# Attention scores of two heads side by side on TensorE's row groups, with a longer lead of the query scores

## The chip, the cores and the metric

The kernel runs on one core of one Trainium2 chip. The metric is the device time of one execution in microseconds (us); three runs of a kernel are given with their median.

## The reference

A macaron layer on x of shape 8 x 256 x 128 (2048 tokens of 128 features, fp32): half a mixture-of-experts stage, an attention, and half a second expert stage with the same weights.

```
ffn(x):  p = softmax(x @ w_gate + b_gate);  e = argmax(p)          # 8 experts, one per token
         y = relu(x @ W1[e] + b1[e]) @ W2[e] + b2[e];  return y * max(p)      # 128 -> 512 -> 128
attn(x): xn = x * rsqrt(mean(x*x) + 1e-6) * norm_w
         q, k, v = xn @ Wq.T + bq, xn @ Wk.T + bk, xn @ Wv.T + bv   # 16 heads of 8 features
         s = q @ k.T / sqrt(8), -inf above the diagonal             # 256 x 256 for each head
         return xn + softmax(s) @ v @ Wo.T + bo
x = x + 0.5 * ffn(ln(x));  x = x + attn(ln(x));  x = x + 0.5 * ffn(ln(x))    # ln: layer norm
```

## The kernel before

**Stages.** A first expert stage, the projections to queries, keys and values, the attention, the routing of the second expert stage (which begins beside the end of the attention), and the second expert stage with POOL's indirect DMAs (dispatch, L479). Each engine has its own instruction list in an order written out by hand; semaphores join them.

**Split numbers.** Queries and keys are split into three bf16 parts each, so that a bf16 product over 6 x 8 = 48 rows (BLK x HD = JROWS) gives a head's score to nearly fp32 precision. Two heads lie above each other in the 96 rows (SROWS) of the stack buffers qz and ks, which SP loads from DRAM (stack_load, L395) with four DMAs for each half of a sequence. In qz the rows of the other head hold zeros, so that a product over 96 rows gives one head. There are two pairs of stack buffers, one for each of two sequences.

**Steps and units.** The attention goes through 16 steps: 8 sequences, each in two halves of 8 heads. This document numbers them 0 to 15; step n is half n % 2 of sequence n // 2. A step has six units u = 0 to 5. A unit fills one PSUM bank of 128 x 512 twice over: with key-major scores (scores_k, L1410) of this step, and with query-major scores (scores_q, L1383) of the step two later, which serve to find each query's row maximum. Units 0, 1, 3 and 4 hold the first 128 keys of a pair of heads against all 256 queries (and the last 128 queries against all keys); units 2 and 5 hold the remaining 128 x 128 blocks of four heads.

**The way of a maximum.** In the query scores TensorE first writes the causal mask into the bank as a product of the identity with a mask table (L1393, L1401), then adds the scores (L1396, L1405). VectorE takes the maximum along the keys (max_unit, L1049, one tensor_reduce of 128 x 512 for a unit). After six units POOL splits the 16 maxima of a query into three bf16 parts (max_split, L544, five small operations), TensorE transposes them into bank 6 (turn_max, L1453, after unit 2), ScalarE copies them to mT (L753), and SP writes them by DMA as three more rows of qz (max_rows, L408). Key scores are a product over these 99 rows, so the maximum is already subtracted in the bank.

**The way of the scores.** ScalarE takes the exponential of a key-score bank to the SBUF tile pT (exp_unit, L740); the two key-score banks alternate. POOL zeroes the entries above the diagonal with affine_select (mask, L562): four masks of 128 x 512 in a step, each after the units that it covers (units 0 and 1; 2; 3 and 4; 5). TensorE multiplies with the values (pv, L1431): part 0 (units 0 to 2) stands after unit 4, part 1 (units 3 to 5) after unit 1 of the next step. An exponential waits until the P·V that read its pT slot before is done. POOL also carries three residual operations (residual, L512, 128 x 256) for each sequence: after masks 1 and 3 of an even step and mask 1 of an odd step (RES_AT, L62).

**The output of a sequence**, one sequence later: ScalarE's out_copy (L755); TensorE's turn_out (L1461) after units 4 and 5 of the even step, into banks 7 and 6; VectorE's normalise (L1094) after unit 5 of the even and unit 0 of the odd step; turn_norm (L1469) after unit 2 and project (L1475) after unit 4 of the odd step; VectorE's add_out (L1104) after its unit 5. VectorE also spreads the values of the next sequence (v_spread, L1088) in the even step. add_out of sequences 0 to 7 is what the second routing (layer norm, gate products, route pick, slots) starts from; late_routing (L1524) puts TensorE's part of it into steps 14 and 15. POOL's first dispatch stands behind its masks of step 15.

**Banks.** 0 and 1 query scores, 2 and 3 key scores, 4 and 5 P·V, 6 and 7 the transposes and projections.

**Loops.** Steps 2 to 9 run in a hardware loop of two turns on every engine; POOL has a small operation in front of each mask there ("turn", L569).

The core of TensorE's step:

```
for u in range(6):
    scores_k(b, k, half, u)
    if more: scores_q(b + 1, bh, 1 - k, half, u)
    if u == 1 and half: pv(b, k, 0, 1)
    elif u == 1 and not first: pv(b - 1, 1 - k, 1, 1)
    if u == 2: ...turn_max...
    if u == 4: pv(b, k, half, 0)
```

Of the kernel before, what the change touches and what calls it, by code (L numbers as in the profile page):

```python
# [67 lines left out]
SROWS = 2 * JROWS  # L68
MROW = SROWS
KROWS = MROW + 3  # L70
NEG1_PAIR = -1082081408
LN_EPS, RMS_EPS = 1e-5, 1e-6
NEG = -1e30
SCALE = 1.0 / float(np.sqrt(np.float32(HD)))
# [28 lines left out]
def build(nc, x_in, wqkvo, cols_in, rows_in, w_gate, experts_in, const_in, out):  # L103
    ctx = ExitStack()
    with ctx:
# [40 lines left out]
        gT = sb("gT", [P, 2, 512])  # L146
# [33 lines left out]
        low = sb("low", [P, P])  # L180
        xs_sb = sb("xs_sb", [P, RING, RW])
# [9 lines left out]
        xnT = sb("xnT", [P, 2, 4 * P])  # L191
        qkr = sb("qkr", [P, 2, 2, 4 * P])
# [8 lines left out]
        mb = sb("mb", [P, 2, 2, 3, 8], BF16)  # L201
        turn = sb("turn", [P, 4])
# [67 lines left out]
        x_ld = sems("x_reloaded", NQ)  # L270
# [13 lines left out]
        low_s = sem("keep_table_set")  # L284
        q_std = sems("sequence_splits_stored", B)
        a_va = sem("attn_v_spread")
        a_stk = [sems(f"stack_loaded{i}_", 2) for i in range(2)]
# [20 lines left out]
        def need(eng, s, n):  # L308

            if not isinstance(n, int) or n > 0:  # L310
                eng.wait_ge(s, n)
# [8 lines left out]
        def scattered(f, k, n):  # L320

            return 16 * (f * len(range(k, NS, OUT)) + n)

# [17 lines left out]
        def _(sp):  # L341
# [53 lines left out]
            def stack_load(b, k, half):  # L395

                r0 = b * (2 * t_rows)
                if half == 0:
                    sp.wait_ge(q_std[b], 64)
                need(sp, a_st, 12 * (b - 2) + 6 * half + 6)  # L400
                for j in range(2):
                    rows_j = slice(JROWS * j, JROWS * (j + 1))
                    for t, buf in ((0, qz[k][rows_j, half, j, :, :]),
# [4 lines left out]
            def max_rows(b, k, half):  # L408

                sp.wait_ge(a_mtc, 2 * b + half + 1)  # L410
                sp.dma_start(qz[k][MROW:MROW + 3, half, :, :, :].rearrange("s j i n -> s (j i n)"), mT[:, half, :]
                             ).then_inc(a_m[half], 16)
# [3 lines left out]
            for q in range(NQ):  # L416
                sp.dma_start(x[:, 4 * q:4 * q + 4, :], tok_view(x_d, q)).then_inc(x_ld[q], 16)
            sp.wait_ge(static_s, 6)
            split_stores(0, 1)
            stack_load(0, 0, 0)  # L420
            stack_load(0, 0, 1)
            stack_load(1, 1, 0)
            max_rows(0, 0, 0)
# [18 lines left out]
        def _(pool):  # L442
# [134 lines left out]
            def step(b, half, more=True):  # L577
                if half == 0:
                    max_split(b, 1)
                elif more:  # L580
                    max_split(b + 1, 0)
# [1044 lines left out]
```

## Time and profile before

| | before |
|---|---|
| median of 3 runs | 317.94 us (317.46 to 318.11) |
| profiled execution | 317.4 us, span 315.3 us |
| TensorE busy | 271.4 us (86%) |
| VectorE busy | 212.2 us (67%) |
| POOL busy | 185.7 us (59%) |
| ScalarE busy | 149.2 us (47%) |

The span runs from the first to the last instruction of the profiled execution; its own time is what that execution took as a run. "Busy" is the time in which an engine computes; waiting and issuing are not in it. PE is TensorE, DVE VectorE, ACT ScalarE, POOL GpSimd, SP the queue that issues most DMAs. PEclk is the granted clock of TensorE as a share of full speed. In a row in order of time the first two numbers are the start and the length of an instruction in us; matmuls are pipelined, so their lengths overlap and the distance from start to start is what one costs its engine. "xN" joins N instructions to one row. Step 0 starts at 123.58 us, step 2 at 137.05, step 13 at 212.28, step 14 at 219.33.

### The profile page before, as it was taken

The page shows a single profiled execution, that of the slowest core. Times are in us where ns is not written, and L with a number is a line of the kernel's source. Part 1 is how long each engine was busy: PE and PEld are TensorE (multiplying, and loading weights), DVE is VectorE, ACT ScalarE, POOL GpSimd, SP SyncE. Part 2 cuts the span into 40 slices and gives each one's busy share as a digit, 9 for nine tenths or more (in the row PEclk, how much of TensorE's full clock was granted, in tenths as well). Part 3 has the DMA queues.
Part 4 walks back from the last instruction along what each step waited for, and adds up shares of the span by engine and source line. Part 5 has one row for each costly group of instructions (what it writes and reads, how often), then busy time and mean ns, then how long its engine had stood idle before and what let it go on. Part 6 is the DMA issues. An engine that isn't in the chain of part 4 may idle for free.

```text
span 315.3 us, 7921 instructions
## 1 busy us (share of the span) xinstructions
PE 271.4 (86%) x2368; PEld 219.5 (70%) x2368; DVE 212.2 (67%) x685; ACT 149.2 (47%) x362; POOL 185.7 (59%) x332
## 2 busy tenths in 40 slices
PE   7724999999997778999989999998977759999980
PEld 6724999999994544656656565665646658999970
DVE  4956058888539568986657777776587744888860
ACT  2300076666206613676656667666541007666620
POOL 7587815445726313786767787888647740555561
PEclk9999999999999996999999999999976799999997
DMA  6974232221041733552433522110001143122100
GB/s 184 397 313 122 60 80 55 68 67 32 17 133 41 202 109 112 165 166 87 135 95 115 157 74 70 58 55 2 5 10 45 56 113 91 49 68 67 30 21 0
DMA packets 34388, 29.37 MB, mean 93 GB/s; under 512 B 4109, under 2 KB 28818, under 8 KB 34353
## 3 DMA queue, kind: packets, MB, share of 16 engines
q1 hardware_dynamic: 29696, 23.52, 25.1%
q0 software_dynamic: 2496, 4.27, 4.3%
q10 hardware_dynamic: 2160, 1.14, 1.4%
q8 instruction: 18, 0.29, 0.4%
q14 instruction: 18, 0.14, 0.1%
HBM read 17.08 MB, written 12.55 MB: 94 GB/s over the span
## 4 chain that ended last, share of the span: by engine, by line
PE 48%; POOL 16%; issue 9%; DMA 9%; DVE 9%; SPq 4%; ACT 2%; POOLq 1%; ACTq 0%; DVEq 0%
PE bank L1291 12%; PE bank L1302 11%; POOL disp_d L479 7%; PE bank L1448 4%; PE bank L1420 3%; PE bank L1396 3%; POOL pT L574 2%; PE bank L1426 2%; DMA row<-in_x 2%; PE bank L1393 2%; SPq L406 2%; POOL row L470 2%; PE bank L1283 2%; PE bank L1401 2%; DMA disp_d<-row,slot 2%
## 5 line engine op out<-in xcount | busy, mean ns | idle before, releaser
L746 ACT ACTIVATE pT<-bank 128x512 f32<-128x512 f32 x96 | 56.5, 600 | 43.0 <-PE bank L1426 29.2
L1056 DVE TENSOR_REDUCE mh<-bank 128x2 f32<-128x512 f32 x64 | 42.1, 683 | 10.1 <-PE bank L1396 9.9
L1302 PE MATMUL bank<-experts,hT 128*128 x368 | 48.9, 276 | 0.0
L1291 PE MATMUL bank<-xsT,ew 128*128 128x128 f32 x368 | 48.8, 276 | 0.1
L1222 PE MATMUL bank<-zero 128*128 128x128 f32 x268 | 37.3, 305 | 10.5 <-DVE rowi L934 4.7
L574 POOL TENSOR_SCALAR_AFFINE_SELECT pT<-pT 128x512 f32<-128x512 f32 x62 | 40.2, 651 | 9.4 <-ACT pT L746 9.3
L1302 PEld LDWEIGHTS bank<-experts,hT 128*128 128x128 f32 x368 | 44.8, 192 | 0.5 <-issue 0.3
L1291 PEld LDWEIGHTS bank<-xsT,ew 128*128 128x128 f32 x368 | 44.7, 192 | 0.5 <-issue 0.2
L1222 PEld LDWEIGHTS bank<-zero 128*128 128x128 f32 x268 | 35.8, 219 | 11.0 <-DVE rowi L934 4.7
L664 ACT ACTIVATE hT<-bank,ew 128x128 f32<-128x128 f32 x92 | 28.9, 365 | 28.7 <-PE bank L1291 28.7
L941 DVE TENSOR_SCALAR hT<-bank,ew 128x128 f32<-128x128 f32 x92 | 28.0, 346 | 21.3 <-PE bank L1291 19.9
L479 POOL DMA_INDIRECT disp_d<-row,slot x32 | 32.3, 1009 | 13.3 <-issue 13.3
L487 POOL DMA_INDIRECT out<-ys_sb,xs_sb x23 | 22.6, 983 | 29.2 <-DVE ys_sb L965 27.7
L487 POOL DMA_INDIRECT x_d<-ys_sb,xs_sb x23 | 22.8, 991 | 24.1 <-DVE ys_sb L965 22.8
L652 ACT ACTIVATE xq<-xs_sb 128x128 f32<-128x128 f32 x46 | 22.5, 492 | 28.8 <-DMA xs_sb<-disp_d 28.8
L1060 DVE TENSOR_REDUCE mh<-bank 128x4 f32<-128x512 f32 x32 | 22.1, 690 | 19.3 <-PE bank L1405 19.3
L1420 PE MATMUL bank<-qz,ks 99*128 99x512 bf16 x64 | 24.8, 390 | 1.9 <-DMA qz<-mT 1.7
L1396 PE MATMUL bank<-ks,qz 96*128 96x256 bf16 x128 | 25.4, 281 | 0.0
L949 DVE TENSOR_SCALAR ew<-experts 128x644 f32 x46 | 22.4, 494 | 2.4 <-issue 1.8
L1448 PE MATMUL bank<-pT,va 128*32 128x256 f32 x256 | 20.9, 398 | 1.8 <-DVE pT L1182 1.5
L957 DVE TENSOR_TENSOR yb<-bank,ew 128x128 f32<-128x128 f32 x46 | 13.4, 292 | 12.8 <-PE bank L1302 10.0
L1393 PE MATMUL bank<-cb 128*128 128x256 bf16 x64 | 18.1, 283 | 1.6 <-DMA ks<-sp_d 1.3
(140 smaller groups left out, 465.9 us busy)
## 6 DMA issues: line engine op xcount, KB each, us to landing
sp_d<-spl SPq DMA_DIRECT2D x32, 192.0 KB, 2.5
experts<-in_experts SPq DMA_DIRECT2D x8, 578.0 KB, 9.5
qz<-sp_d SPq DMA_DIRECT2D x32, 96.0 KB
ks<-sp_d SPq DMA_DIRECT2D x32, 96.0 KB
xs_sb<-disp_d SPq DMA_DIRECT2D x46, 66.0 KB, 1.9
row<-in_x SPq DMA_DIRECT2D x4, 256.0 KB, 5.2
row<-x_d SPq DMA_DIRECT2D x4, 256.0 KB, 3.6
disp_d<-pad ACTq DMA_DIRECT2D x12, 66.0 KB
```

The lines of the kernel that those rows point to most:

```text
L479: pool.indirect_dma_start(disp_d[f][:, :], bass.IndirectOffsetOnAxis(ap=slot[:, t:t + 1], axis=0), row[:, t, :], None).then_inc(d_tok[f], 16)
L487: pool.indirect_dma_start(target[:, :], bass.IndirectOffsetOnAxis(ap=xs_sb[:, t % RING, ID:ID + 1].bitcast(U32), axis=0), ys_sb[:, t % OUT ...
L574: pool.affine_select(out=p_, in_=p_, pattern=[[0, 4], [1, P]], compare_op=ALU.is_ge, fill=0.0, base=0, channel_multiplier=-1).then_inc(a_p ...
L664: mm = act.activation(hT[:, par, c, :], bank[2 + 2 * par][:, c * P:(c + 1) * P], ACT.Relu, bias=ew[:, k, HID + c:HID + c + 1])
L746: act.activation(pT[:, u, :], bank[2 + u % 2][:, :], ACT.Exp, scale=SCALE).then_inc(a_e, 1)
L1056: dve.tensor_reduce(mh[:, half, 1, :, 2 * pp + w], bank[u % 2][:, :].rearrange("p (h n) -> p h n", h=2), AX.X, ALU.max).then_inc(a_mx, 1)
L1222: pe.matmul(bank[b][:, 0:P], zero[:, :], zero[:, :], start=True, stop=True)
L1291: mm = pe.matmul(bank[2 + 2 * (k % 2) + c // 2][:, (c % 2) * P:(c % 2 + 1) * P], ew[:, k % WRING, c * P:(c + 1) * P], xsT[:, k % 2, :], st ...
L1302: mm = pe.matmul(bank[6 + k % 2][:, 0:D], hT[:, k % 2, c, :], w2.rearrange("p a c -> p (a c)"), start=(c == 0), stop=(c == HC - 1))
L1396: mm = pe.matmul(ov[:, j, :], qz[k][0:SROWS, half, j, pair - 4 * half, P:T], ks[k][0:SROWS, pair, :], start=False, stop=True, **MM_BANK)
L1420: mm = pe.matmul(ov, ks[k][0:KROWS, pair, 0:P], qz[k][0:KROWS, half, :, pair - 4 * half, :], start=True, stop=True, **MM_BANK)
L1448: mm = pe.matmul(o[32 * h:32 * h + 32, pp * T:(pp + 1) * T], va[:, k, 0, 8 * j + pair, :], pT[:, 3 * pp + h // 2, j * T:(j + 1) * T], star ...
```

## The change

**Row groups.** The two heads of a pair no longer share rows: head 0 lies at partitions 0 to 47, head 1 at 64 to 111, each followed by its own three rows of maxima (48 to 50, 112 to 114; max_rows becomes two DMAs). A product is over 48 or 51 rows, and a unit now interleaves a key-score product of one row group with a query-score product of the other (scores). The zeros in qz are dropped. Units 2 and 3 are now the ones with 128 x 128 blocks of four heads, units 0, 1, 4 and 5 the wide ones with two products each.

**Lead.** Three pairs of stack buffers, three query banks (0, 1, 6). From step 2 on a step computes the query scores of step n + 3 (QUERY_OF); between steps 1 and 2 the query half 4 is computed alone (scores_alone); steps 13 to 15 have none. The row maxima are turned two steps ahead (MAX_OF), after unit 3.

**Mask.** In the wide units, from sequence 1 on, the mask product is dropped; VectorE adds the mask from a table msk and takes the maximum in one operation (tensor_tensor_reduce, 128 x 256, two for a unit). Units 2 and 3, and all units of sequence 0, keep the mask product and tensor_reduce.

**Moves.** P·V part 0 stands after unit 5 and waits for three masks, part 1 for all five; POOL has five masks (three of 512 columns, two of 256) and a max_split of four operations; its residual stays behind masks 1, 3 and 1. Bank 6 being a query bank, turn_out uses bank 7 twice: first query block after unit 5 of the even step, second after unit 1 of the odd step, where it waits for normalise of the first. turn_norm, project and add_out follow at units 0, 1 and 2 of the next even step. The maxima's transposes use bank 7. One value-bias addition (quad_vbias(3)) and the mask table go to VectorE's prologue. All loops are unrolled and the turn operations dropped.

```diff
@@ constants
-KROWS = MROW + 3
+KROWS = JROWS + 3
+JBASE = P // 2
+QB = (0, 1, 6)
+QUERY_OF = [n + 2 if n < 2 else n + 3 for n in range(HALVES - 3)] + [None] * 3
+MAX_OF = [n + 1 if n < 2 else n + 2 for n in range(HALVES - 2)] + [None] * 2
...
-        qz = [sb(f"qz{i}", [P, 2, 2, 4, T], BF16) for i in range(2)]
-        ks = [sb(f"ks{i}", [P, NPAIR, T], BF16) for i in range(2)]
+        qz = [sb(f"qz{i}", [P, 2, 4, T], BF16) for i in range(3)]
+        ks = [sb(f"ks{i}", [P, NPAIR, T], BF16) for i in range(3)]
...
@@ POOL
+            def mask(n, i):
+                pool.wait_ge(a_e, 6 * n + (2, 3, 4, 5, 6)[i])
...
+                pool.affine_select(out=p_, in_=p_, pattern=[[0, 2 if i > 2 else 4], [1, P]], compare_op=ALU.is_ge,
+                                   fill=0.0, base=0, channel_multiplier=-1).then_inc(a_pm, 1)
+            def step(n):
...
+                for i in range(5 if n < HALVES - 1 else 2):
+                    mask(n, i)
...
+                    elif (half, i) in RES_AT:
+                        residual(b, RES_AT.index((half, i)))
@@ ScalarE, exp_unit
-                need(act, a_pv, 2 * (2 * b + half - 1) + 1 + u // 3
+                need(act, a_pv, 2 * (2 * b + half - 1) + (1 if u < 2 else 2)
@@ VectorE, max_unit
+                if b == 0 or late:
+                    i1 = dve.tensor_reduce(top, bank[QB[u % 3]][:, :].rearrange("p (h n) -> p h n", h=heads),
+                                           AX.X, ALU.max)
...
+                    for m in range(heads):
+                        sc = bank[QB[u % 3]][:, m * n:(m + 1) * n]
+                        i1 = dve.tensor_tensor_reduce(sc, sc, msk[:, T - n:T], 1.0, LOWEST, ALU.add, ALU.max,
+                                                      top[:, m:m + 1])
@@ VectorE, step
+                    if (half, u) == (0, 2):
+                        if b >= 2:
+                            add_out(b - 2)
+                        v_spread(b + 1, (b + 1) % 2)
...
+                        if (half, u) == (1, 0):
                             normalise(b - 1, 0)
-                        if half == 1 and u == 0:
+                        if (half, u) == (1, 2):
                             normalise(b - 1, 1)
@@ TensorE
+            def scores(n, mq, u):
+                if u == 0:
+                    pe.wait_ge(a_m[n % 2], 32 * (n // 2 + 1))
+                need(pe, a_e, 6 * n + u - 1)
+                if mq is not None:
+                    scores_q_waits(mq, u)
+                    masked = mq < 2 or unit(u)[0]
+                    if masked:
+                        scores_q_mask(u)
+                for m in range(unit(u)[2]):
+                    mm = scores_k_part(n, u, m)
+                    if mq is not None:
+                        mm_q = scores_q_part(mq, u, m, masked)
...
             def pv(b, k, half, pp):
-                pe.wait_ge(a_pm, 8 * b + 4 * half + 2 * pp + 2)
+                pe.wait_ge(a_pm, 5 * (2 * b + half) + 3 + 2 * pp)
...
             def step(n):
                 for u in range(6):
+                    scores(n, QUERY_OF[n], u)
+                    if (half, u) == (0, 0) and b >= 2:
+                        turn_norm(b - 2)
+                    if u == 1 and n > 0:
+                        pv(b if half else b - 1, b % 2 if half else 1 - b % 2, 1 - half, 1)
+                    if (half, u) == (0, 1) and b >= 2:
+                        project(b - 2)
+                    if u == 3 and MAX_OF[n] is not None:
...
+                        turn_max(MAX_OF[n])
+                    if u == 5:
+                        pv(b, b % 2, half, 0)
...
+                    if (half, u) == (0, 5) and 1 <= b and not last:
+                        pe.wait_ge(a_mtc, MAX_OF[n] + 1)
+                        turn_out(b - 1, 0)
+                    if (half, u) == (1, 1) and 1 <= b and not last:
+                        pe.wait_ge(a_an, 2 * b - 1)
+                        turn_out(b - 1, 1)
+                    if last:
+                        if (half, u) == (0, 4):
+                            pe.wait_ge(a_x, b - 1)
+                            turn_out(b - 1, 0)
+                        if (half, u) == (1, 0):
+                            pe.wait_ge(a_an, 2 * b - 1)
+                            turn_out(b - 1, 1)
...
+            for u in range(6):
+                scores_alone(4, u)
```

## Rows read from the trace of the kernel before

**Rows 1.** Busy time of each engine in four stretches; columns in its first line.

```profile
...
core 0: us, PE busy (x) PEld busy (x) DVE busy (x) ACT busy (x) POOL busy (x), PEclk, DMA share, GB/s
123.58:137.05 13.47, 13.08 (x122) 8.01 (x121) 11.93 (x19) 8.95 (x16) 9.58 (x21) 0.88 0.61 176
137.05:212.28 75.23, 73.23 (x783) 46.24 (x784) 53.88 (x116) 47.96 (x94) 57.60 (x153) 1.00 0.34 100
212.28:219.33 7.05, 6.51 (x72) 4.17 (x70) 4.78 (x11) 4.20 (x9) 5.64 (x13) 1.00 0.01 2
219.33:233.44 14.11, 12.09 (x123) 8.07 (x124) 9.87 (x40) 8.53 (x18) 7.80 (x17) 0.97 0.01 3
```

**Rows 2.** Waits, 137.05 to 212.28 us: waiter, releaser, us, times, longest.

```profile
...
ACT pT L746 <- PE bank L1426: 18.9, 23, 1.0
...
PE bank L1420 <- DMA qz<-mT: 1.7, 1, 1.7
```

**Rows 3.** TensorE in order of time, steps 2 and 3: start, us, line, operation.

```profile
...
138.09 0.38 PE L1396 MATMUL bank<-ks,qz 96*128 96x256 bf16 x2
138.41 0.64 PE L1448 MATMUL bank<-pT,va 128*32 128x256 f32 x8
138.86 0.40 PE L1444 MATMUL bank<-pT,va 128*32 128x128 f32 x8
139.20 0.39 PE L1426 MATMUL bank<-qz,ks 99*128 99x256 bf16 x2
139.43 0.38 PE L1401 MATMUL bank<-cb 128*128 128x512 bf16 x1
...
142.19 0.66 PE L1465 MATMUL bank<-ident_t,oT 128*128 128x128 f32 x4
142.68 0.38 PE L1426 MATMUL bank<-qz,ks 99*128 99x256 bf16 x2
...
149.25 0.71 PE L1478 MATMUL bank<-wt,anT 128*128 128x128 f32 x4
149.79 0.39 PE L1426 MATMUL bank<-qz,ks 99*128 99x256 bf16 x2
```

**Rows 4.** VectorE in order of time, from 143 to 153 us.

```profile
...
143.55 0.69 DVE L1060 TENSOR_REDUCE mh<-bank 128x4 f32<-128x512 f32 x1 [1.04 <-PE bank L1405]
144.16 0.25 DVE L1098 RECIPROCAL rl<-bank 128x16 f32<-128x16 f32 x1
144.44 0.29 DVE L1100 TENSOR_TENSOR an<-bank,rl 128x128 f32<-128x128 f32 x1
...
151.27 0.41 DVE L1107 TENSOR_TENSOR row<-bank,row 128x256 f32 x1
151.60 1.28 DVE L1056 TENSOR_REDUCE mh<-bank 128x2 f32<-128x512 f32 x2
```

**Rows 5.** ScalarE and POOL in order of time, step 3.

```profile
...
143.10 0.60 ACT L746 ACTIVATE pT<-bank 128x512 f32<-128x512 f32 x1 [0.84 <-PE bank L1426]
...
143.78 0.20 POOL L569 TENSOR_TENSOR turn<-zero 128x1 f32<-128x1 f32 x1 [0.58 <-ACT pT L746]
143.93 0.64 POOL L574 TENSOR_SCALAR_AFFINE_SELECT pT<-pT 128x512 f32<-128x512 f32 x1
...
144.53 0.72 POOL L521 TENSOR_TENSOR res<-res,rows 128x256 f32<-128x256 f32 x1
...
145.21 0.22 POOL L552 TENSOR_TENSOR mb<-mh,zero 128x16 bf16<-128x16 f32 x1
```

**Rows 6.** VectorE and POOL in order of time, steps 14 and 15 and after.

```profile
...
220.14 0.41 DVE L1107 TENSOR_TENSOR row<-bank,row 128x256 f32<-128x256 f32 x1
...
227.11 0.22 DVE L861 TENSOR_TENSOR lg<-bank,row 128x64 f32<-128x64 f32 x1 [1.20 <-PE bank L1252]
...
229.84 0.25 DVE L1098 RECIPROCAL rl<-bank 128x16 f32<-128x16 f32 x1
...
233.44 1.09 POOL L479 DMA_INDIRECT disp_d<-row,slot  x1 [1.78 <-issue]
```

More of the change, by code:

```diff
@@ L577, in step @@
[L577 to L581, printed above, removed]
-                for n in range(4 if more or half == 0 else 2):
-                    mask(b, half, n // 2, n % 2)
-                    if isinstance(b, int) and b >= 6:
-                        if b == 6 and n > 0:
-                            residual(6 + half, n - 1)
-                    elif (half, n) in RES_AT:
-                        residual(b, RES_AT.index((half, n)))
-                    if isinstance(b, int) and b >= 5 and (half, n) == (0, 1):
+                z_ = zero[:, 0:16].rearrange("p (q j h) -> p q j h", q=2, j=2)
@@ L594, in _ @@
             quad_repeat(4, 1)
-            for half in range(2):
-                if half == 1:
-                    quad_repeat(4, 0)
-                step(0, half)
-            with pool.Fori(0, 2) as i:
-                for k in range(2):
-                    for half in range(2):
-                        step(2 * i + 1 + k, half)
-            for b in (5, 6, 7):
-                for half in range(2):
-                    step(b, half, more=b < 7)
+            step(0)
+            quad_repeat(4, 0)
+            step(1)
+            max_split(3)
+            for n in range(2, HALVES):
+                step(n)
             dispatch(1, 0, range(0, 3))
@@ L785, in _ @@
             quad_split2(4)
-            step(0, 1, True, first=True)
-            with act.Fori(0, 2) as i:
-                for k in range(2):
-                    for half in range(2):
-                        step(2 * i + 1 + k, half, True)
-            for b in (5, 6, 7):
-                for half in range(2):
-                    step(b, half, b < 7)
+            step(1)
+            max_copy(3)
+            for n in range(2, HALVES):
+                step(n)
             out_copy(7, 1)
@@ L1148, in _ @@
             for u in range(6):
-                max_unit(0, 1, u)
+                max_unit(1, u)
             v_spread(0, 0)
-            for half in range(2):
-                step(0, 0, half, True, first=True)
-            with dve.Fori(0, 2) as i:
-                for k in range(2):
-                    for half in range(2):
-                        step(2 * i + 1 + k, 1 - k, half, True)
-            for b in (5, 6):
-                for half in range(2):
-                    step(b, b % 2, half, True)
+            step(0)
+            step(1)
+            for u in range(6):
+                max_unit(4, u)
+            for n in range(2, HALVES - 2):
+                step(n)
+            add_out(5)
             def late_stats(q):
@@ new lines, in scores_q_waits, with scores_q_part @@
+                    pe.wait_ge(a_stk[mq // 2 % 3][mq % 2], 64 * (mq // 6 + 1))
+                need(pe, a_mx, 6 * mq + u - 2)
+            def scores_q_part(mq, u, m, masked=False):
+                late, p0, heads = unit(u)
+                n = 512 // heads
+                q_, k_ = head(mq // 2 % 3, mq % 2, p0 + m, 1 - u % 2, JROWS)
+                return pe.matmul(bank[QB[u % 3]][:, m * n:(m + 1) * n], q_[:, 0:P] if late else q_[:, P:T], k_[:, 0:n],
+                                 start=not masked, stop=True, **(MM_BANK if masked else {}))
@@ L1518, in step @@
                             turn_norm(b - 1)
[L1519 removed]
+                        if (half, u) == (1, 4):
                             project(b - 1)
[L1521 removed]
                         late_routing(half, u)
```

411 lines of the change are left out of this document (191 added, 220 removed).

## The prediction

> **What bounds the kernel now.** I read the busy shares first, then busy time by stretch, then the waits, then TensorE, VectorE and POOL in order of time. TensorE is busy 86% of the span, but the stretch decides, not the share. Steps 2 to 12 of the attention (a step is one half of the heads of one sequence) take 75.23 us, TensorE is busy in 73.23 of them, and VectorE, ScalarE and POOL in 46 to 58 [rows 1]. The 2.0 us without TensorE are nearly all one wait of 1.7 for the row-maximum transfer; ScalarE's exponentials wait 18.9 us for TensorE's scores [rows 2]. So 75.23 − 1.7 = 73.5 us over 11 steps is 6.68 a step, set by TensorE's stream. The changed kernel takes work out of that stream; the question is what is late next. Behind the attention POOL's dispatches and the second expert stage run in series, so what comes late at the first dispatch (233.44 [rows 6]) comes late at the end.
>
> **TensorE's stream.** Two products of 256 columns take .23 (139.20 to 139.43 [rows 3]), so one takes .11. A unit (key scores, mask, query scores) costs .34 to .45 of it now. Side by side on two row groups it costs .22, and .44 where the mask stays (units 2 and 3). That is 4 × .22 + 2 × .44 = 1.76 a step in place of about 2 × (.22 + .34 + .22 + .34 + .22 + .45) = 3.6, or 1.8 less. The trace has no pair on two row groups. Its nearest case is eight products of 256 columns on four column groups that take .45 (138.41 to 138.86 [rows 3]) where eight in turn would take .9; so tiles do run beside each other, and I take the full overlap. The other bound is none.
>
> **What a step waits for then.** I cost the 1.8 at nothing gained by itself and follow the chain, since P·V of units 0 and 1 now stands after unit 5 and needs three POOL masks, and the exponentials of the next step's units 0 and 1 need that P·V. Prices: P·V .79 (138.41 to 139.20), turn_out .49 (142.19 to 142.68), turn_norm half of that, .25, project .54 (149.25 to 149.79), score start to exponential .42 and so .20 after a .22 unit, all [rows 3] with the exponential at 143.10 [rows 5]; exponential .60 long, .08 to POOL's next start (143.70 to 143.78), mask .60 start to start and .64 long, residual .68 (144.53 to 145.21) [rows 5]; normalise .28 + .29 [rows 4]. A switch between the tile shapes: P·V starts at 138.41, the two products before it end at 138.09 + .22 = 138.31, so .10 [rows 3].
>
> *Odd step, from its first score:* two units .44, P·V .79: 1.23. turn_out of the second query block now shares bank 7 with the first and waits for VectorE's normalise, which stands behind unit 0's maximum: .42 + two reduces of .42 (below) + .57 + .05 = 1.88. Queued behind that wait on TensorE is unit 2, and behind it exponential 2. turn_out to 2.37; unit 2 with mask and switch .54, 2.91; exponential 3.11 to 3.71; second mask 3.79; residual 4.39, third mask 5.07 to 5.71; P·V 5.76 to 6.55.
>
> *Even step:* .22 + .25 + .22 + .79 + .54 = 2.02; unit 2 to 2.56; exponential 2.76 to 3.36; mask 3.44, residual 4.04, mask 4.72 to 5.36; P·V 5.41 to 6.20; turn_out 6.69.
>
> Six even and five odd steps: 6 × 6.69 + 5 × 6.55 = 72.9, 2.3 less than 75.23, nearly all of it the transfer wait, which two steps' lead should remove. A stream that one engine sets hides its hand-overs, this chain has them bare; I add .10 a step, the size of the .08 and .10 above: +1.1. The residual is not moved, but until now it lay beside TensorE's work; on this chain it costs .68 a step.
>
> [...] The Trainium skill, TensorEngine Tiling (Array Packing), Key Properties, says that a change of the tiling mode drains TensorE and that changing only the tile does not. By that rule each masked unit drains once in and once out, which my sum charges once; charging both would add .10 × 11 = 1.1 us; the trace agrees that there is a gap, and shows it in one direction only.
>
> **VectorE.** The new fused add-and-maximum (128x256 from PSUM and SBUF) is not in the trace. Below it is bounded by half a 512-wide reduce of .61 (143.55 to 144.16), .30, above by a whole one, .60. Nearest is add_out: 128x256, PSUM and SBUF in, .33 start to start, .41 long [rows 4]. Since the new one also writes its accumulator, I take the length, .42. A pair of steps then holds 16 × .42 + 4 × .61 + about 2.05 (two normalise, add_out, v_spread) = 11.2, below the chain's 13.2: hidden at .42, no longer at .55.
>
> **Steps 0, 1 and the extra half.** The lead of three halves is bought by six query units alone between steps 1 and 2. VectorE is the bound there already: 11.93 of 13.47 busy [rows 1], of which 12 × .61 = 7.3 are maxima. After: 4.6 other work less .6 (one bias addition goes to the prologue) + 16 × .42 + 4 × .61 = 13.2; then unit 5 of the extra half may be issued when unit 2's maximum is done: 4 × .42 + .61 + .22 = 2.5. That is 15.7 for 13.47: +2.2 (−0.2 at .30, +5.8 at .60). The clock is .88 there [rows 1]; if TensorE, idle behind VectorE, is given 1.2 GHz again, its .22 become .44, still below VectorE's pace.
>
> **Prologue:** the bias addition .6 on VectorE and a second transfer for the row maxima, about half hidden: +.3 (0 to 1).
>
> **Step 13** has no query scores left: odd step without their mask and without VectorE's wait: 1.23 + .49 + .32 + .20 + .60 + .08 + .60 + .68 + .64 + .05 + .79 = 5.7 for 7.05 [rows 1]: −1.35.
>
> **Steps 14, 15.** add_out of sequence 5 came .81 after step 14's start (220.14 − 219.33 [rows 6]); project now runs in that step, so it comes after 2.02 + .20, 1.4 later. Behind it hang statistics, gate products and the route pick (227.11). I let .9 of it through (0 to 1.4), since the pick also waits 1.20 for TensorE's logits [rows 6]. From the pick's end (229.84) to the first dispatch it was 3.6. Now turn_out waits for the normalise on the one bank, and unit 2 and POOL's second mask, ahead of the dispatch in POOL's queue, wait for it: .57 + .05 + .49 + .22 + .79 + .32 + .20 + .60 + .08 + .64 + about .85 to the dispatch = 4.8, +1.2. Together +2.1.
>
> SP's six issues a step stay hidden below 6.6 us, and POOL loses a split operation and the turn operations (143.78 [rows 5]) and gains a mask; they are in the chain where they count.
>
> **Sum.** +.3 + 2.2 − 2.3 + 1.1 − 1.35 + 2.1 = +2.0 on the profiled execution's 317.4 (span 315.3 and 2.1 around it) gives 319.4; the median of the runs lies .5 above the profiled one: **320.0 us**, slower.
>
> **Rivals.**
> *B, faster:* the chain is shorter than drawn. If TensorE's work ahead of unit 2 overlaps what I put in series (turn_norm and project .79 in the even step; the wait for normalise and turn_out 1.14 in the odd one), 1.3 of a pair goes, the pair takes 11.9, still above VectorE's 11.2: −1.3 × 5.5 = −7.2, 312.8; range 309 to 317. For it: no engine holds more than 11.2 of my 13.2, and TensorE has 1.8 a step to spare. Against: every link is a wait in the code. It decides from .2 a step.
> *C, VectorE the bound:* at .60, a pair takes 16 × .60 + 2.4 + 2.05 = 14.1, +.86 over mine, 5.5 × .86 = 4.7, and steps 0, 1 and the extra half 20 × .18 = 3.6: 328.3. Against: the .33 row. The Trainium skill, same page, PSUM Bottleneck, warns that tiling speeds up TensorE but not the reading of PSUM, which may then bind; no run here shows it yet.
> *D, no overlap of row groups* (the change doesn't do what it says): units 0 to 2 each .22 longer on the chain, .66 × 11 = 7.3: 327.3. Against: the .45 row.
>
> **Chances.** Forecast .48 (own range 316 to 325), B .35, C .10, D .07. About ±.2% (.64 us) can be told from no change: faster .03 + .32, same .06 + .03, slower .56. Range: 310 leaves the lowest fifth of B out, 328 half of C and some of D, together under .2.
>
> **What would show it.** TensorE's busy time in steps 2 to 12 falls by some 20 us while the stretch stays 72 to 75; ScalarE waits for unit 2, POOL for ScalarE, and TensorE's longest waits are on POOL's third mask and on normalise; the fused reduce's price is read start to start; the wait for the row maxima is gone; the extra half costs 2 to 3 us. A stretch near 66 would prove B, VectorE without gaps C, units of .44 D.

## The result, and the profile after

The changed kernel takes 354.80 us (median of four runs, 350.91 to 357.18) where the kernel before takes 317.94: a ratio of 1.108, 95% interval 1.101 to 1.114. It was forecast slower, at 320.0 with 310 to 328 as range: the sign was right, the size was not. The ratios leave out executions that took over 1.5% more than the fastest of their kernel, the medians do not, so the two need not agree. The runs of the changed kernel lie 6 us apart, those of the kernel before .7 (4.7 in the 29 runs of it beside e13 to e16); the profiled execution is the longest of the four (357.18), with a span of 354.8 us, 39.5 more than before. So the stretches below add up to more than the ratio does: the two executions that it counts take 5 us less (350.91 and 353.29). The lower clock is in all four: .835 to .863 of full speed over the whole span, where the kernel before was granted .961 (.901 to .962 in those 29).

The page of the changed kernel, TensorE's busy share and granted clock in 40 slices of 8.9 us:

```profile
...
PE   7808999999886999498886768768969688999990
...
PEclk9999999999999556756999988896655658999995
...
```

From the fourteenth slice on (115 us) TensorE is granted half speed, with breaks, until 296 us; before the change it stood at 1.00 through steps 2 to 13 [rows 1]. By stretch (the last 9.9 us of the prologue, up to step 0, which starts at 129.15; steps 0, 1 and the extra half; steps 2 to 12; step 13; steps 14 and 15 up to the first dispatch), the changed kernel:

```profile
core 0: us, PE busy (x) PEld busy (x) DVE busy (x) ACT busy (x) POOL busy (x), PEclk, DMA share, GB/s
119.25:129.15 9.90, 9.51 (x35) 2.99 (x34) 7.81 (x12) 2.45 (x4) 1.96 (x7) 0.50 0.06 15
129.15:150.90 21.75, 16.06 (x150) 7.61 (x147) 17.92 (x61) 8.87 (x17) 12.88 (x29) 0.66 0.52 153
150.90:241.93 91.03, 70.97 (x823) 35.74 (x824) 60.41 (x247) 45.78 (x93) 53.30 (x120) 0.84 0.25 74
241.93:249.17 7.24, 5.65 (x56) 2.51 (x55) 1.10 (x4) 3.86 (x8) 4.25 (x10) 0.74 0.01 2
249.17:271.67 22.50, 18.79 (x128) 11.53 (x124) 8.20 (x34) 7.06 (x14) 5.97 (x12) 0.58 0.00 1
...
```

Against [rows 1]: step 0 starts 5.6 later (129.15 − 123.58), steps 0 and 1 take 8.3 more (with the extra half), steps 2 to 12 15.8, step 13 .2, steps 14 and 15 8.4 (14.1 before), what follows 1.3: 39.5 in all. The waits of the changed kernel over the whole span (us in total, times, longest):

```profile
...
ACT pT L753 <- PE bank L1421: 77.6, 42, 4.3
...
PE bank L1476 <- POOL pT L587: 13.6, 15, 2.1
...
PE bank L1421 <- DMA ks<-sp_d: 6.5, 3, 2.6
...
```

The wait for the row maxima [rows 2] is gone; three waits for stack loads have come. What one of them does, on TensorE in order of time at step 9 of the changed kernel:

```profile
...
203.26 0.64 PE L1476 MATMUL bank<-pT,va 128*32 128x256 f32 x8 [0.72 <-POOL pT L587]
203.72 0.40 PE L1471 MATMUL bank<-pT,va 128*32 128x128 f32 x8
204.05 0.66 PE L1494 MATMUL bank<-ident_t,oT 128*128 128x128 f32 x4
...
207.21 0.27 PE L1421 MATMUL bank<-qz,ks 51*128 51x256 bf16 x1 [2.50 <-DMA ks<-sp_d]
...
208.03 1.08 PE L1476 MATMUL bank<-pT,va 128*32 128x256 f32 x8
208.88 0.65 PE L1471 MATMUL bank<-pT,va 128*32 128x128 f32 x8
...
```

Eight P·V products take .46 us ahead of the wait (203.26 to 203.72) and .85 behind it (208.03 to 208.88): the clock went from 2.4 to 1.2 GHz (granted 1.00 over 197.50 to 207.21, .75 over 207.21 to 214.50).

At full clock the steps are as forecast. Steps 5, 6 and 7 of the changed kernel:

```profile
...
176.03:182.51 6.48, 4.87 (x72) 2.60 (x73) 5.29 (x21) 4.03 (x8) 3.98 (x9) 1.00 0.22 65
182.51:191.03 8.52, 5.99 (x82) 3.22 (x79) 5.34 (x22) 4.25 (x9) 5.77 (x16) 1.00 0.51 144
191.03:197.50 6.47, 4.87 (x72) 2.61 (x73) 5.27 (x21) 4.03 (x8) 3.31 (x6) 1.00 0.21 62
...
```

```profile
...
185.35 0.22 PE L1421 MATMUL bank<-qz,ks 51*128 51x128 bf16 x1
...
185.50 0.39 PE L1427 MATMUL bank<-cb 128*128 128x512 bf16 x1
185.83 0.23 PE L1421 MATMUL bank<-qz,ks 51*128 51x128 bf16 x1
...
191.03 0.27 PE L1421 MATMUL bank<-qz,ks 51*128 51x256 bf16 x1 [1.32 <-DMA ks<-sp_d]
...
```

The stretch of the even step ends with 1.32 us of waiting for a load, so a pair is 6.48 + 7.20 = 13.7 (13.24 + .2 forecast). The even step is .4 longer than forecast and the odd one .2 shorter, so the pair is right in part by offset. Ahead of unit 2 the even step takes 2.35 us (182.51 to 184.86) for 2.02. The gap of about .10 at a switch of tile shape, which the forecast charged once for a masked unit, shows on both sides of the mask product: 185.41 to 185.50 and 185.72 to 185.83, with .06 and .22 for the products themselves. The fused operation on VectorE, in order of time:

```profile
...
183.32 0.47 DVE L1073 CUSTOM_DVE_ANT_0 bank<-bank,msk 128x256 f32<-128x256 f32 x1
183.70 0.14 DVE L1073 DVE_READ_ACCUMULATOR2_ANT mh<- 128x1 f32 x1
183.70 0.47 DVE L1073 CUSTOM_DVE_ANT_0 bank<-bank,msk 128x256 f32<-128x256 f32 x1
...
```

It costs .38 from start to start, with a second instruction that reads the accumulator beside the next one (.42 charged).

### The profile page after: what moved, and what is told of

It is laid out like the page before. It is cut to its first block, busy times and chain, and to the rows that moved or that the text cites. A ratio compares the mean times of both kernels' runs of the same rounds, so it can differ in the third digit from the quotient of the medians.

```text
span 354.8 us, 7968 instructions
## 1 busy us (share of the span) xinstructions
PE 289.7 (82%) x2440; PEld 214.2 (60%) x2440; DVE 220.6 (62%) x855; ACT 146.4 (41%) x362; POOL 177.8 (50%) x298
## 3 DMA queue, kind: packets, MB, share of 16 engines
q10 hardware_dynamic: 2160, 1.14, 1.2%
## 4 chain that ended last, share of the span: by engine, by line
PE 45%; POOL 15%; issue 14%; DVE 12%; DMA 6%; SPq 3%; ACT 2%; POOLq 1%; DVEq 0%; ACTq 0%
PE bank L1305 11%; PE bank L1316 10%; POOL pT L587 6%; PE bank L1236 4%; PE bank L1476 3%; PE bank L1421 3%; DMA ks<-sp_d 2%; POOL disp_d L495 2%; PE bank L1413 2%; PE bank L1494 2%; PE bank L1427 2%; DVE bank L1073 2%; PE bank L1471 1%; DMA row<-in_x 1%; PE bank L1297 1%
## 5 line engine op out<-in xcount | busy, mean ns | idle before, releaser
L587 POOL TENSOR_SCALAR_AFFINE_SELECT pT<-pT 128x512 f32<-128x512 f32 (+1 forms) x77 | 42.8, 561 | 55.8 <-ACT pT L753 55.4
L1073 DVE CUSTOM_DVE_ANT_0 bank<-bank,msk 128x256 f32<-128x256 f32 x112 | 44.5, 451 | 19.9 <-PE bank L1413 19.2
L1236 PE MATMUL bank<-zero 128*128 128x128 f32 x268 | 39.5, 317 | 7.9 <-DVE rowi L943 4.6
L1421 PE MATMUL bank<-qz,ks 51*128 51x256 bf16 (+1 forms) x256 | 39.6, 282 | 6.9 <-DMA ks<-sp_d 6.5
L1236 PEld LDWEIGHTS bank<-zero 128*128 128x128 f32 x268 | 37.9, 230 | 8.4 <-DVE rowi L943 4.7
L1413 PE MATMUL bank<-ks,qz 48*128 48x256 bf16 (+1 forms) x256 | 40.4, 287 | 0.0
L1476 PE MATMUL bank<-pT,va 128*32 128x256 f32 x256 | 27.6, 514 | 14.4 <-POOL pT L587 13.6
L1067 DVE TENSOR_REDUCE mh<-bank 128x4 f32<-128x512 f32 (+1 forms) x40 | 27.0, 686 | 19.0 <-PE bank L1413 19.0
L495 POOL DMA_INDIRECT disp_d<-row,slot x32 | 31.5, 983 | 11.7 <-issue 11.7
L1421 PEld LDWEIGHTS bank<-qz,ks 51*128 51x128 bf16 x256 | 16.8, 102 | 25.6 <-issue 22.6
L1413 PEld LDWEIGHTS bank<-ks,qz 48*128 48x128 bf16 x256 | 17.3, 103 | 6.9 <-issue 5.7
```

Source lines behind the costliest of these rows:

```text
L495: pool.indirect_dma_start(disp_d[f][:, :], bass.IndirectOffsetOnAxis(ap=slot[:, t:t + 1], axis=0), row[:, t, :], None).then_inc(d_tok[f], 16)
L587: pool.affine_select(out=p_, in_=p_, pattern=[[0, 2 if i > 2 else 4], [1, P]], compare_op=ALU.is_ge, fill=0.0, base=0, channel_multiplier= ...
L1073: i1 = dve.tensor_tensor_reduce(sc, sc, msk[:, T - n:T], 1.0, LOWEST, ALU.add, ALU.max, top[:, m:m + 1])
L1236: pe.matmul(bank[b][:, 0:P], zero[:, :], zero[:, :], start=True, stop=True)
L1413: return pe.matmul(bank[QB[u % 3]][:, m * n:(m + 1) * n], q_[:, 0:P] if late else q_[:, P:T], k_[:, 0:n], start=not masked, stop=True, **( ...
L1421: return pe.matmul(bank[2 + u % 2][:, m * n:(m + 1) * n], k_[:, P:T] if late else k_[:, 0:P], q_[:, T - n:T], start=True, stop=True)
```

## The experiments

Two theories: the *waits* cost what they last; or each longer wait also halves TensorE's *clock*, and the work behind it takes twice as long. All kernels but the last two are versions of the changed one. The table has the median and the interval of the ratio to the kernel before, and then four pieces of the profiled span: up to the first P·V of step 0; from there to the first P·V in step 2 (steps 0, 1 and the extra half); from there to P·V part 0 of step 12, with the granted clock; and from there to the first dispatch, with the clock.

| | us | ratio | start | to step 2 | to step 12 | to dispatch |
|---|---|---|---|---|---|---|
| before | 317.9 | | 128.4 | 10.0 | 71.5 (1.00) | 23.6 (.98) |
| changed | 354.8 | 1.101 to 1.114 | 134.4 | 17.5 | 87.6 (.85) | 32.2 (.61) |
| e1 | 352.3 | 1.097 to 1.111 | 134.2 | 24.1 | 77.3 (.95) | 31.8 (.58) |
| e2 | 352.8 | 1.098 to 1.115 | 128.9 | 16.6 | 87.7 (.81) | 33.0 (.60) |
| e3 | 345.5 | 1.073 to 1.090 | 130.0 | 19.1 | 80.8 (1.00) | 28.3 (.75) |
| e4 | 355.1 | 1.106 to 1.120 | 132.6 | 25.9 | 79.5 (.92) | 31.3 (.70) |
| e5 | 346.3 | 1.081 to 1.097 | 134.2 | 15.3 | 80.2 (.90) | 31.4 (.62) |
| e6 | 339.0 | 1.063 to 1.072 | 131.4 | 14.7 | 73.1 (.90) | 32.6 (.69) |
| e7 | 330.4 | 1.033 to 1.039 | 130.5 | 14.7 | 73.7 (.90) | 29.0 (.74) |
| e8 | 360.1 | 1.129 to 1.139 | 129.9 | 14.4 | 99.6 (.75) | 29.5 (.76) |
| e9 | 325.3 | 1.020 to 1.030 | 129.3 | 14.8 | 67.3 (.98) | 26.2 (.77) |
| e10 | 320.2 | .998 to 1.007 | 129.1 | 15.1 | 64.9 (.97) | 27.6 (.68) |
| e11 | 331.7 | 1.036 to 1.052 | 129.9 | 14.8 | 71.6 (1.00) | 26.3 (.81) |
| e12 | 325.0 | 1.007 to 1.022 | 129.1 | 14.7 | 72.7 (.91) | 26.6 (.82) |
| e13 | 317.3 | .995 to 1.002 | 129.0 | 14.7 | 65.1 (.95) | 23.9 (.86) |
| e14 | 318.0 | .994 to 1.000 | 129.3 | 15.1 | 64.5 (1.00) | 23.9 (.93) |

**e1, loads first, and e5, the same again.**

```diff
             for n in range(2, HALVES):
-                if MAX_OF[n] is not None:
-                    max_rows(MAX_OF[n])
                 if n in stores:
                     split_stores(stores[n])
                 if n + 5 < HALVES:
                     stack_load(n + 5)
+                if MAX_OF[n] is not None:
+                    max_rows(MAX_OF[n])
```

> The changed kernel with one thing moved: SP issues the stack loads of a step ahead of its row-maximum transfers instead of behind them (and stack_load 5, whose buffers are free from the start, beside stack_load 4). Theory of the waits (TensorE loses just what it waits for): the three waits of TensorE for ks<-sp_d (2.6, 1.3 and 2.5 us) go, 6.5 us less, about 347 us. Theory of the clock (each such gap also lets TensorE's clock fall to 1.2 GHz for the 8 to 12 us behind it): the steps behind the gaps get full clock too, 3 to 4 us more for each of them, about 336 to 341 us.

> The changed kernel with SP's stack loads ahead of the row-maximum transfers from step 2 on, and with stack_load 5 beside stack_load 4, both behind the transfer of maxima 1 (in e1 stack_load 4 stood ahead of it and blocked it for 6.8 us, which hid the result). Theory of the clock: no gap of 1.3 us or more in steps 2 to 9, these at 6.8 us each at full clock; the gaps of ln_scale (steps 10, 12) and the slow steps behind them stay: steps 2 to 12 about 80 us for 91, prologue and end as in the changed kernel, about 343 us. Theory of the waits: 6.5 less, 347 us.

e1 came out above both forecasts. It moved stack_load 4, which waits for its split store, ahead of the maxima of step 1, and TensorE stood 6.8 us for them. Its middle (from step 2 to step 12) still fell by 10.3, where only 3.8 us of the waits for loads (1.32 + 2.50) lay. e5, without that fault, came to a ratio of 1.089 for 1.108, about 6 us less, and no more than the 6.5 waited for: its 346.3 lies nearer to the waits' 347 than to the clock's 343. Its middle fell by 7.4. But both middles are set against the longest execution of the changed kernel, so up to 5 us of such a fall can be chance, and neither run parts the theories.

**e2, POOL's order.**

```diff
                 for i in range(5 if n < HALVES - 1 else 2):
                     mask(n, i)
-                    ...residual and ln_scale between the masks...
+                for op in ((0, 1), (2,))[half]:
+                    residual(b, op)
+                if b in (5, 6) and half == 0:
+                    ln_scale(2, b - 5)
```

> The changed kernel with POOL's residual operations, and ln_scale in steps 10 and 12, moved behind the last mask of their step. Theory of the waits: .68 us off the way to the third mask in each of 11 steps and 2 x 1.4 us of ln_scale, about 10 us less, 345 us. Theory of the clock: the two gaps of 2.1 us before P.V in steps 10 and 12 no longer halve the clock, some 5 us more, 340 us; the transfers' gaps are still there. If POOL's order is not on the chain: no change.

A miss: the whole hardly moved. Where the clock was full, P·V part 1 to part 0 fell from 4.74 (e1) to 4.08 us, about the .68 of the residual, so POOL's order is on the chain. But the shorter steps met the loads earlier: TensorE waited for them four times, 11.0 us in all (longest 3.8), where the changed kernel waits 6.5 in three. And VectorE's ln_bias now waited for the later ln_scale.

**e3, fillers, and e4, all three.**

```diff
+            def fill(n, count):
+                if count:
+                    need(pe, a_ot, n - 1)
+                for _ in range(count):
+                    pe.matmul(bank[4 + n % 2][:, 0:P], zero[:, :], zero[:, :], start=True, stop=True)
```

> The changed kernel with all its waits, and dummy products of zeros added on TensorE in the places where it waits (before the first unit of steps 2, 7 and 9, before P.V part 0, before the maxima's transposes and before the second turn_out; they write columns that P.V overwrites). They do no work that anyone needs. Theory of the waits: not faster, 355 us or slower. Theory of the clock: steps 2 to 12 fall from 91 us to about 82 (75.6 of chain at full clock, 3.8 of transfers, 2.8 of ln_scale), granted clock above .95 there, about 343 to 347 us.

> Loads first, POOL's residual and ln_scale last, and the small fillers (none at the first unit) together. Theory of the clock: steps 2 to 12 at full clock without transfers' waits and without residual on the chain, 11 x 6.2 to 6.3 = 68 to 70 us for 91, about 328 to 334 us. Theory of the waits: 6.5 + 10 less and the fillers' cost on top, about 338 to 342 us.

e3 removes nothing that TensorE waits for and is faster by about 8 us (1.081 for 1.108), as the theory of the clock had it (343 to 347); one of its four executions took 379.95. Its middle is at full clock throughout:

```profile
core 0: us, PE busy (x) PEld busy (x) DVE busy (x) ACT busy (x) POOL busy (x), PEclk, DMA share, GB/s
149.09:229.88 80.79, 78.26 (x946) 49.25 (x944) 60.07 (x247) 45.26 (x93) 50.79 (x114) 1.00 0.27 82
...
```

The theory of waits cannot give that: its time was 355 or slower, and the products are work that nobody needs. How much they gained is less sure: the middle is 6.8 us shorter than in the longest execution of the changed kernel, and the start, which has no filler, is 4.4 shorter too. e4 was a miss: it carries e1's fault at the start, and where the waits are gone the fillers stand on the chain (4.67 us from part 1 to part 0 of P·V, where e2 has 4.08).

**e6 to e9, the parts together.** e6 is e5 with e2's POOL order; e7 adds the end's order and idle work at the start; e8 is e7 with a lead of two; e9 is e7 with ln_bias a step later.

```diff
# e7
+                    if n == 13 and u == 4: ...turn_norm(5)      # project(5) behind unit 5
-                            pe.wait_ge(a_an, 2 * b - 1)
+                        if (half, u) == (0, 5):
                             turn_out(b - 1, 1)                  # bank 6 for b >= 6
# e8
-QUERY_OF = [n + 2 if n < 2 else n + 3 for n in range(HALVES - 3)] + [None] * 3
+QUERY_OF = [n + 2 for n in range(HALVES - 2)] + [None] * 2
+MAX_OF = [n + 1 for n in range(HALVES - 1)] + [None]
# e9
-                        if (half, u) == (0, 5):
+                        if (half, u) == (1, 5):
                             ln_bias(2, b - 5)
```

> e5 with POOL's residual and ln_scale behind the last mask (e2), no fillers. In e2 the full-clock pairs took about 12.1 us, in e1 13.6. Theory of the chain: steps 2 to 12 take 5.5 x 12.1 = 67 us, 24 less than the changed kernel, about 331 us in all, if the clock stays up. Theory that TensorE, now idle for a larger share, loses its clock without any long gap: pairs of 13.5 to 16 us, 340 us or more.

> e6 with the end as the kernel before has it: turn_norm and project of sequence 5 in step 13, the second turn_out of sequences 6 and 7 in bank 6 (free there) in place of waiting for the normalise of the first; and six more calls of idle work ahead of the first query scores, where TensorE waits 1.5 us for the first stack load. Steps 14 and 15 up to the first dispatch: 22.5 us in the changed kernel, 14.1 before. Theory of the order (project late, one bank): 15 to 16 us, 7 less, and 3 to 5 less in the prologue if that gap is what lowers the clock there: about 320 us. Theory that the end is only slow from the clock: the order gives 2, the rest stays, about 328 us.

> e7 with the lead of the query scores back to two halves in all steps, so without the extra query half between steps 1 and 2 (9 to 15 us between P.V of step 1 and of step 2 in the traces so far, 3.1 before), and with the row maxima turned one step ahead. If the extra half is only paid for and the longer lead buys nothing on the chain: 5 to 7 us less than e7 (one step's query scores more in step 13), about 314 us, below the kernel before. If the lead of three is needed, the wait for the maxima's transfer returns, .5 us or more a step, and it is no faster than e7.

> e7 with VectorE's ln_bias of steps 10 and 12 one step later (it waits for POOL's ln_scale, which e2, e6 and e7 put at the end of the step, so that VectorE stood there for 2.5 and 3.7 us and TensorE behind it for 3.0 and 2.3). Theory of the clock: these were the last long gaps, so steps 11 to 13 run at full clock at 6.2 us as steps 4 to 10 do, some 8 to 10 us less than e7, 320 to 322 us. Theory of the waits: 5 less, 325 us.

e6 took 339.0 for the 331 of its chain. Its pairs from step 4 to step 10 take 12.4 us at full clock, so TensorE's smaller busy share did not lower the clock there, as its other forecast had it (pairs of 13.5 to 16); but two long waits were left. They were left in e7 too, which at 330.4 lies above both its forecasts (320 and 328): TensorE stood 3.04 us at 204.96 for a normalise behind ln_bias, and the clock halved behind it. e9 takes that away: pairs of 12.4 us and a middle of 67.3. Its whole, 325.3, is what the waits alone give (325) and not what the clock's theory did (320 to 322); a wait of 2.85 us in step 13 for POOL's split of the maxima was left, and .69 was granted from there to the first dispatch. e8 was a miss of mine: in this order the lead is needed. Its waits from 125 to 262 us:

```profile
...
PE bank L1421 <- DMA qz<-mT: 20.8, 12, 5.2
...
```

SP itself stood 57.2 us for the copies of the maxima in that time, so they are late, and not SP's order.

**e10 to e12, what the chain is made of.**

```diff
# e10, steps 2 to 12
-                    if (half, u) == (0, 1) ...: project(b - 2)
+                    if (half, u) == (0, 3) ...: project(b - 2)
-                    if (half, u) == (1, 1) ...: turn_out(b - 1, 1)
+                    if (half, u) == (1, 3) ...: turn_out(b - 1, 1)
-                    if u == 3 ...: turn_max(MAX_OF[n])
+                    if u == 5 ...: turn_max(MAX_OF[n])
# e11
-                    masked = mq < 2 or unit(u)[0]
+                    masked = True
# e12: all scores_k_part of a unit, then all scores_q_part
```

> e9 with TensorE's side work of steps 2 to 12 moved to where it waits anyway: project and the second turn_out behind unit 3, the maxima's transposes behind unit 5 ahead of P.V. Theory of the chain: .54 of project (even steps) and .9 of turn_out and its wait (odd steps) stood ahead of unit 2, on the way to the third mask; off it, about .5 to .7 us a step, 5 to 8 us less than e9, near 314. If the chain is set elsewhere (VectorE, POOL): no change.

> e9 with all masks of the query scores on TensorE and VectorE's maxima all by tensor_reduce, as before the change. A wide unit then costs TensorE about .12 us more and VectorE .16 less (.61 for 2 x .385). If VectorE's fused operation bounds the steps: faster than e9 by up to 5 us. If TensorE stands on the chain ahead of unit 2 (units 0 and 1): .25 us a step more, 3 us slower than e9, and 1 us less in the extra query half.

> e9 with a unit's key-score products issued before its query-score products instead of in turns, so that a pair on two row groups can overlap only where the two groups meet. If row groups do run beside each other, a wide unit goes from .23 to about .34 us and a step's way to unit 2 is longer by some .3, 3 to 4 us slower than e9. If they do not, no difference.

e10 took 5.1 us off e9 by the medians and about 7 by the ratios, of the 5 to 8 forecast. Its pairs take 11.4 to 11.7 us, two later ones 12.9 and 12.3, so what stands ahead of unit 2 on TensorE is on the chain. In e11 a pair takes 13.6 for 12.4 although VectorE is busy for less (51.75 us of the middle for 57.41): VectorE is not the bound. The whole is 6 us slower than e9, for 3 forecast. e12 decides nothing: it is not slower than e9 (325.0 for 325.3), which was to mean that row groups do not overlap. Its middle is longer by 5.4 at .91 granted, but its pairs at full clock are e9's, and its rows show why the order of issue makes no difference here (both key products are issued first, L1426 is key, L1418 query):

```profile
...
179.97 0.28 PE L1426 MATMUL bank<-qz,ks 51*128 51x256 bf16 x1
179.98 0.28 PE L1418 MATMUL bank<-ks,qz 48*128 48x256 bf16 x1
180.09 0.27 PE L1426 MATMUL bank<-qz,ks 51*128 51x256 bf16 x1
180.10 0.37 PE L1418 MATMUL bank<-ks,qz 48*128 48x256 bf16 x2
...
```

A kernel without overlap was not made, so what the overlap itself is worth was not measured.

**e13 and e14, the end and the start.** e13 is e10 with residuals of sequences 6 and 7 in steps 13 and 14; e14 adds fillers at the start.

```diff
# e13
-                if b == 6: ...residual(6 + half, op)
+                if n in (13, 14): ...residual(n - 7, op)
# e14
+            idle_work(1, 2)            # ahead of turn_max(0); idle_work(7, 4) ahead of unit 3
+                    fill(1, 5)         # ahead of P.V of step 1; fill(2, 6) ahead of step 2
```

> e10 with POOL's residual operations of sequences 6 and 7 one step later (steps 13 and 14), so that max_split of step 13 no longer stands behind them and TensorE no longer waits 1.8 us for it. Theory of the clock: that wait is what halves the clock for the whole end (.65 granted over the last 33 us of the attention in e10, 27.5 us before the change); without it the end takes 28 to 30, about 315 us. Theory of the waits: 1.8 less, 318 us.

> e13 with dummy products where TensorE waits between the first maxima and step 2 (before the first transposes, before unit 3 of the second half, before P.V of step 1, before step 2). Theory of the clock: steps 0 and 1 and the extra half, 20 us at .79 in e10, go to about 17; 2 to 3 us less than e13, near 312, below the kernel before. Theory of the waits: the fillers buy nothing, e13's time or more.

In e13 one wait of 1.8 us is gone and the end is 3.7 us shorter (27.6 to 23.9, clock .68 to .86), which fits the clock; its whole, 317.3, is nearer to what the wait alone gives (318) than to the clock's 315. e14's fillers gained nothing at the start and nothing in all (the clock's theory had 312), and a granted .93 for .86 did not shorten its end, so there the clock no longer sets the time. e13 and e14 are the fastest versions found; neither can be told from the kernel before. Their middle is 6 to 7 us shorter than before, and the extra half (5 us longer to step 2) eats most of it.

**e15 and e16, the same loss idle and busy, in the kernel before.**

```diff
# e15, SP and TensorE in step 10
+                        sp.wait_ge(a_st, 12 * 5 + 3)
+                        sp.dma_start(scratch[:, :], zero[:, 0:4]).then_inc(pause, 16)
+                        pe.wait_ge(pause, 16)
# e16, TensorE in the same place
+                        for _ in range(9):
+                            pe.matmul(bank[4][:, 0:P], zero[:, :], zero[:, :], start=True, stop=True)
```

> The kernel before with one pause: in step 10 TensorE waits after unit 2 for a small transfer that SP issues once that unit's key scores are done; about 2 us without products, in a stretch at full clock. Theory of the waits: 2 us longer than the kernel before (less where other engines catch up). Theory of the clock: the granted clock falls to half behind the pause, as behind the gaps of the changed kernel, for 3.4 us or more; 4 us longer or more.

> The kernel before with the same time lost in the same place of step 10, but with TensorE busy: nine dummy products of .25 us in place of the pause. Both theories: 2.2 us longer than the kernel before, clock 1.00 throughout the step. Set against e15 this parts a wait from what the clock adds to it.

322.3 us (ratio 1.011 to 1.019) against 320.7 (1.006 to 1.012), with 318.1 for the kernel before beside them: 4.2 us longer with the pause (the waits' theory had 2, the clock's 4 or more), 2.6 with the products (2.2 by both). Whole runs part them by 1.6 us, with intervals that touch; the step parts them clearly. e15, the pause with the two P·V around it, and the stretches behind it:

```profile
...
194.25 0.64 PE L1453 MATMUL bank<-pT,va 128*32 128x256 f32 x8
...
198.76 0.61 PE L1425 MATMUL bank<-qz,ks 99*128 99x512 bf16 x1 [2.68 <-DMA scratch<-zero]
...
206.42 0.64 PE L1453 MATMUL bank<-pT,va 128*32 128x256 f32 x8
...
```

```profile
...
190.00:197.00 7.00, 6.07 (x68) 3.60 (x65) 5.22 (x15) 4.56 (x9) 5.37 (x15) 1.00 0.21 64
197.00:201.00 4.00, 2.24 (x8) 1.04 (x8) 0.89 (x5) 1.59 (x3) 1.72 (x3) 0.64 0.09 30
201.00:204.00 3.00, 3.00 (x24) 1.89 (x24) 0.69 (x1) 0.07 (x1) 0.64 (x1) 0.50 0.02 5
204.00:207.00 3.00, 3.00 (x31) 2.10 (x31) 2.05 (x7) 1.74 (x3) 2.08 (x6) 0.84 0.18 49
...
```

And e16 in the same stretches, then its two P·V, and those of the kernel before:

```profile
...
190.00:197.00 7.00, 6.98 (x70) 4.84 (x72) 4.66 (x15) 3.56 (x7) 5.56 (x13) 1.00 0.19 60
197.00:201.00 4.00, 4.00 (x51) 2.78 (x55) 2.67 (x7) 2.46 (x5) 2.28 (x5) 1.00 0.08 18
201.00:204.00 3.00, 3.00 (x35) 1.84 (x31) 2.54 (x7) 1.94 (x5) 2.60 (x7) 1.00 0.33 104
...
```

```profile
...
191.85 0.64 PE L1448 MATMUL bank<-pT,va 128*32 128x256 f32 x8
...
200.50 0.64 PE L1448 MATMUL bank<-pT,va 128*32 128x256 f32 x8
...
```

```profile
...
193.68 0.64 PE L1448 MATMUL bank<-pT,va 128*32 128x256 f32 x8
...
200.23 0.64 PE L1448 MATMUL bank<-pT,va 128*32 128x256 f32 x8
...
```

From the P·V before the place to the second one behind it e15 takes 194.25 to 206.42 = 12.2 us, e16 191.85 to 200.50 = 8.7, the kernel before 193.68 to 200.23 = 6.6. A wait of 2.7 us cost 5.6; products that nobody needs in the same place cost 2.1. The two profiled executions, 326.6 and 317.1 us, lie at opposite ends of their runs, so only this stretch is compared: both come to it at a granted 1.00.

Taken together, the theory of the clock gave the direction and not the size. That a wait can cost TensorE's clock, and time beyond its length, is shown by e15 against e16 and by e3. As a forecast of whole times it held in e3 and e15; in e5, e9, e13 and e14 the waits alone came nearer, and e1, e2, e4 and e7 lay above both forecasts.

## Why the prediction was wrong

**Right:** the 1.8 us a step taken out of TensorE's stream do not shorten the step by themselves; row groups do overlap (a pair of products takes .12), which with the fused operation's price (.38 for .42) leaves nothing for the rivals C and D; the chain from exponential over masks to P·V (a pair 13.7 for 13.4); the residual at .68 on it (e2); the side work ahead of unit 2 (e10); the wait for the row maxima gone, and the lead needed for that (e8). The overlap was read from too low a price: eight P·V products in turn were put at .9, the price of bf16, but their rows say f32, and four f32 products of 128 columns take .54 there, so about 2.2 by that row (an estimate). That the kernel is slower was forecast from the extra half (+2.2) and the end (+2.1); most of the rise of a tenth came from elsewhere, so the right sign is in large part luck.

**The step that failed** is "I cost the 1.8 at nothing gained by itself and follow the chain", with every wait charged at its length. Behind its long waits TensorE lost its clock, and then its own work, at twice its price, was the path. The prediction looked at the clock for the extra half alone and let it pass. In steps 2 to 12 the steps at full clock would make 6 × 7.20 + 5 × 6.48 = 75.6; loads (1.32 + 2.50) and ln_scale (2 × 1.4) make 82.2; by subtraction the other 8.8 of the 91.0 come with the half clock, in this execution, and e3, whose waits stay and whose clock does not fall there, is 6.8 shorter in the middle. TensorE's busy time there, which was to fall by some 20 us, fell by 2.3 (73.23 to 70.97), at .84 granted. The low clock is in the other stretches too, but there its part was not measured: the end is 8.4 longer for 2.1 forecast, at .58 granted; the prologue 5.6 for .3, at .50; step 13 .2 longer for 1.35 shorter, at .74.

**Second,** "a transfer wait which two steps' lead should remove" and "SP's six issues a step stay hidden": the loads that step n + 2 needs stood behind the row maxima of step n and the split stores in SP's queue, and came 1.3 to 2.6 us late at the start of steps 2, 7 and 9; with them put ahead (e5), the kernel took about 6 us less. I counted SP's issues, not when the first of them could go.

**Third,** POOL's ln_scale (1.27 us in step 10, from 221.43 to the third mask at 222.70) in steps 10 and 12 was left out of the chain, though it stands in the code beside the residual that was counted. With it TensorE waited 2.1 us for the mask (.72 in step 8, which has none). With it and the residual behind the last mask (e6) the kernel took about 7 us less than e5.

**Mis-sized:** the extra half, +2.2 forecast, costs about 5 in the best versions (to step 2: 15 for 10 us), and 7.5 in the changed kernel. The clock of the changed kernel falls already at 115 us, behind a wait of 1.50 for the first stack load. In e1, e4, e5 and e6 this wait was 1.14 to 1.33, and the clock fell there too; in e2 and e3 (.86 and .75) and in e7, where idle work fills it (.24), it held past 121 us. But the kernel before waits 1.32 there and also held until 120, so the length of the wait alone does not say it, and that stays open.

## What to carry to other kernels

Work taken off TensorE is not free time if TensorE then waits: look at its longest single waits, and at the granted clock behind each, before at its busy share. When an engine stops being the bound, lay out the new chain through every queue it crosses, with each instruction that stands in that queue in each step, unrolled ends included. A filler pays where the wait can't be removed, and costs where it can.

## What the runs showed of the hardware

A wait of 2.68 us on TensorE alone in a full-clock stretch was followed by half clock (e15), one of 1.32 (step 7 of the changed kernel) was not, nor one of 1.69 in the kernel before (159.10, for the row maxima). Two of nearly one length went both ways: behind 1.80 us in e2 (185.24) the clock stayed at 1.00, behind 1.83 in e10 (214.38) it fell to .50. Products of two row groups ran beside each other although both of one group were issued first (179.97 and 179.98 in e12).
